# Softmax attention: which PSUM banks hold the maxima and which the scores, and where a step's side work stands

## The chip, the cores and the metric

The kernel runs on one core of a Trainium2 chip, in one launch. The metric is the device time in microseconds (us), the median of the runs.

## What is computed

The reference is a two-layer model; only its first attention matters here. For x of 8 x 512 x 128 (normalised by rows first), with 16 heads of 8:

```
q, k, v = split_heads(binlinear(x, Wq, bq)), ...      # binarised weights
att = softmax(einsum('bhtd,bhsd->bhts', q, k) * 8 ** -0.5)
y = einsum('bhts,bhsd->bhtd', att, v)                 # then binlinear(y, Wp, bp)
```

Behind it come a routed expert layer (8 experts, the best 2 of each token), a second attention with squared scores, and a coupling network.

## The kernel before

The attention is `attention0`. Its work is cut into **128 steps** (`LAST`), 16 for each of the 8 batch elements (`b` is the element, `t` the step in it). A quad is four heads (`GH = 4`) of one element; four steps make a quad, and step `s` handles one tile of 128 keys of it. The stacked queries and keys of a quad's four heads lie in four strips of 32 partitions, so that matmuls of the four heads use four different row strips of TensorE.

Each step has these parts:

- **maxima** (`maximum`, L616 to L627): TensorE computes the scores of 128 queries against all 512 keys, a bank of PSUM for each head, and VectorE reduces each to the negated maximum of every query (L1042). They run `AHEAD = 6` steps ahead of the scores. When a quad's 16 maxima are there VectorE transposes them (`turn`, L1047), and SyncE copies them into an extra row of the stacked queries (`max_rows`, L333), so that the scores come out with the maximum taken off.
- **scores** (`scores`, L629 to L641): 128 keys against 512 queries, one matmul for a head; ScalarE's exponential (L819) reads them.
- **weights** (`weigh`, L650 to L663): the exponentials of two steps before (`LAG = 2`) times the values, summed into the bank `av`, 4 heads beside each other, in two parts.
- **side work** at fixed steps: the gather of the sums by head at t = 2 and 4 (`gather`, L674), the turn of the normalised values at t = 6 (`turn_y`, L686), the output projection at t = 8 (L694), the projections of the queries and keys three elements ahead at t = 10 and 12 (`q_k`, L579), the next values at t = 14 (`values`, L587), and once each the router's gates, logits and counts. ScalarE reads each of them out.

A step is two halves, which TensorE issues as (`group`, L643 to L647, and the loop from L758): maximum, two scores, maximum; weights part 0; maximum, two scores, maximum; side work; weights part 1. A group with what follows it up to the next group is called a **half-step** here.

PSUM has eight banks: three take the maxima in turn (`max_banks`: bank0, bank1, misc), four (`quad`) hold scores in two pairs, and one is `av`. The pairs are used by units, numbered in the order of their issue in the table `units`: a unit is two scores or one piece of side work, and takes a pair. `wait_bank` (L287) makes TensorE wait until the unit two before has been read; ScalarE reads a pair of scores with one exponential of 1024 elements. `unit_read` counts what ScalarE has read, `max_free` what VectorE has reduced.

```
wait(pe, max_free, n - 2)        # maximum n: the bank of maximum n - 3 has been reduced
wait(engine, unit_read, n - 1)   # unit n: the pair of unit n - 2 has been read
```

The chain from a gather to the turn of the values: ScalarE copies the gathered sums (L857), VectorE inverts the denominators (`invert_sums`, L1059) one step after the gather and behind that step's maxima, GpSimd multiplies (`scale_rows`, L521), and then `turn_y` may start (it waits for `yn_done`). ScalarE reads `av` into `osb` (`read_o`, L826) at the ends of t = 1 and t = 9; gather and weights wait for that (`o_read`).

## Time and profile before

| | |
|---|---|
| median of 3 runs (lowest to highest) | 981.44 us (981.0 to 982.44) |
| the profiled execution, its own time | 983.3 us |
| its span | 981.5 us |
| PE busy | 894.2 us (91%) |
| DVE busy | 679.1 us (69%) |
| ACT busy | 633.1 us (65%) |
| POOL busy | 380.9 us (39%) |
| exponentials, L819 | 257.3 us in 256 |
| maxima on DVE, L1042 | 337.5 us in 512 |

The shares are over the whole program; the attention's steps lie between 50 and 416 us of the span. PE is TensorE (PEld its weight loads), DVE VectorE, ACT ScalarE, POOL GpSimd. The two groups of maxima (the banks, 222.0 us, and misc, 115.5 us) are added in the last line. A busy PE counts every matmul from its start to its modelled end, so matmuls of different row strips that run together count once, and a PE that looks busy may still be waiting.

### The profile page before, as it was taken

To read this page: it belongs to the slowest core of one execution; us is meant where nothing else is said; L and a number is where in the kernel's file an instruction comes from. 1 tells how busy PE (TensorE), PEld (TensorE's weight loads), DVE (VectorE), ACT (ScalarE), POOL (GpSimd) and SP (SyncE) were. 2 spreads that over 40 slices of the span, in tenths; PEclk is the share of its full clock that TensorE was granted. 3 is DMA by queue.
4 is the path that set the end of the run, shared out by engine and by line. 5 is a ranking of instruction groups with operands and counts; after the bars stand their busy time and mean duration, and the time that the engine had idled before them with its cause. 6 is when DMAs were issued, how large, how long until landed. Compare 5 with 4: busy or idle time off the path is not lost. (4 is left out here: it accounts for less than half of the span.)

```text
span 981.5 us, 18238 instructions
## 1 busy us (share of the span) xinstructions
PE 894.2 (91%) x6642; PEld 466.6 (48%) x6642; DVE 679.1 (69%) x1253; ACT 633.1 (65%) x1152; POOL 380.9 (39%) x376
## 2 busy tenths in 40 slices
PE   4699999999999999989898978899689999999997
PEld 2334444444444444468788866322234444434443
DVE  7779989898888998423333358777857667766654
ACT  4568787778787887832222223567567778777875
POOL 4112141325454343015565531455636446644200
PEclk9579999999999999989999989989779999999999
DMA  7715625132323000146666361369977999999700
GB/s 223 258 30 211 238 84 200 64 140 84 116 90 110 27 26 27 51 121 195 200 200 202 107 201 56 87 105 139 137 82 76 102 115 103 103 100 115 87 13 22
DMA packets 81484, 114.03 MB, mean 116 GB/s; under 512 B 14482, under 2 KB 58516, under 8 KB 78964
## 3 DMA queue, kind: packets, MB, share of 16 engines
q1 hardware_dynamic: 74228, 94.62, 48.5%
q0 software_dynamic: 6352, 17.86, 5.3%
q8 instruction: 53, 0.87, 0.4%
q10 hardware_dynamic: 816, 0.39, 0.1%
q14 instruction: 35, 0.29, 0.1%
HBM read 56.00 MB, written 33.57 MB: 91 GB/s over the span
## 5 line engine op out<-in xcount | busy, mean ns | idle before, releaser
L819 ACT ACTIVATE a_probs<-quad 128x1024 f32<-128x1024 f32 x256 | 257.3, 1024 | 58.3 <-PE quad L639 50.7
L1042 DVE TENSOR_REDUCE a_nmax<-bank 128x1 f32<-128x512 f32 x342 | 222.0, 680 | 31.5 <-PE misc L626 16.2
L1909 ACT ACTIVATE a_late<-quad 128x256 f32<-128x256 f32 (+3 forms) x512 | 180.5, 463 | 38.6 <-PE quad L1678 37.6
L2064 DVE SCALAR_TENSOR_TENSOR a_late<-a_late,const 128x512 f32<-128x512 f32 x128 | 117.1, 923 | 76.2 <-ACT a_late L1909 75.9
L659 PE MATMUL av<-a_probs,a_va 128*32 128x256 f32 x2048 | 163.2, 392 | 4.4 <-ACT a_osb L826 4.4
L626 PE MATMUL bank<-k_stack,q_stack 24*128 24x512 f32 x342 | 147.7, 515 | 6.1 <-DVE a_nmax L1042 4.2
L639 PE MATMUL quad<-q_stack,k_stack 25*128 25x512 f32 x512 | 129.8, 502 | 0.3 <-DMA q_stack<-a_ntop 0.3
L1042 DVE TENSOR_REDUCE a_nmax<-misc 128x1 f32<-128x512 f32 x170 | 115.5, 679 | 13.7 <-PE bank L626 12.6
L1678 PE MATMUL quad<-q_stack,k_stack 96*128 96x256 bf16 (+3 forms) x512 | 104.1, 303 | 7.8 <-ACT a_late L1909 4.0
L1689 PE MATMUL av<-a_late,a_va 128*32 128x512 f32 (+3 forms) x1024 | 97.2, 452 | 8.2 <-DVE a_late L2075 7.2
L626 PEld LDWEIGHTS bank<-k_stack,q_stack 24*128 24x128 f32 x342 | 59.5, 188 | 86.4 <-DVE a_nmax L1042 59.3
L514 POOL DMA_INDIRECT sorted_rows<-x_rows,a_slot x64 | 62.5, 976 | 74.3 <-PE av L659 70.6
L626 PE MATMUL misc<-k_stack,q_stack 24*128 24x512 f32 x170 | 87.6, 515 | 1.8 <-DVE a_nmax L1042 1.7
L1407 DVE TENSOR_TENSOR m_hid<-m_act,quad 128x512 f32<-128x512 f32 x55 | 37.4, 684 | 74.5 <-PE quad L1336 31.5
L1678 PEld LDWEIGHTS quad<-q_stack,k_stack 96*128 96x128 bf16 x512 | 44.5, 98 | 88.0 <-ACT a_late L1909 62.2
L1610 POOL TENSOR_TENSOR a_rest<-a_full,a_parts 128x512 f32<-128x512 f32 x32 | 41.4, 1294 | 94.4 <-DVE a_parts L2056 93.5
L659 PEld LDWEIGHTS av<-a_probs,a_va 128*32 128x32 f32 x2048 | 41.2, 108 | 70.1 <-issue 37.7
L1378 ACT ACTIVATE m_act<-bank 128x512 f32<-128x512 f32 x55 | 32.8, 596 | 53.0 <-PE bank L1331 41.2
L1305 POOL DMA_INDIRECT expert_rows<-m_ob,m_xr x50 | 47.8, 957 | 30.8 <-DVE m_ob L1414 18.5
L1373 ACT ACTIVATE m_xt<-quad 128x256 f32<-128x256 f32 x39 | 14.8, 383 | 69.0 <-PE quad L1317 59.6
L626 PEld LDWEIGHTS misc<-k_stack,q_stack 24*128 24x128 f32 x170 | 32.0, 188 | 42.4 <-DVE a_nmax L1042 29.4
L639 PEld LDWEIGHTS quad<-q_stack,k_stack 25*128 25x128 f32 x512 | 47.8, 183 | 6.2 <-ACT a_probs L819 3.3
(288 smaller groups left out, 1390.8 us busy)
## 6 DMA issues: line engine op xcount, KB each, us to landing
spread<-a_parts SPq DMA_DIRECT2D x48, 256.0 KB
q_stack<-a_parts SPq DMA_DIRECT2D x96, 128.0 KB, 7.5
k_stack<-a_parts SPq DMA_DIRECT2D x96, 128.0 KB, 7.7
wu<-packed_weights SPq DMA_DIRECT2D x20, 384.0 KB
m_wu<-packed_weights SPq DMA_DIRECT2D x19, 384.0 KB
q_stack<-spread SPq DMA_DIRECT2D x7, 1024.0 KB
k_stack<-spread SPq DMA_DIRECT2D x7, 1024.0 KB
sorted_rows<-in_shape_constants POOLq DMA_DIRECT2D x5, 1040.0 KB, 6.5
```

Of the source, the lines that this page charges most:

```text
L514: pool.indirect_dma_start(S["sorted"], bass.IndirectOffsetOnAxis(ap=slot[k][:, t:t + 1], axis=0), S["rows"][:, t, :], None).then_inc(done, 16)
L626: pe.matmul(max_banks[n % 3][:, :], qs[b % 4][at, c, qt * P:(qt + 1) * P].bitcast(F32R), ks[b % 4][at, c, :].bitcast(F32R), start=True, st ...
L639: last = pe.matmul(pair_of(n)[:, k, :], ks[b % 4][at, c, kt * P:(kt + 1) * P].bitcast(F32R), qs[b % 4][at, c, :].bitcast(F32R), start=True ...
L659: last = pe.matmul(av[STRIP * j:STRIP * (j + 1), at], va[b % 2][:, kt, GH * j + c, :], probs[:, (GH * s + j) % PROBS, at], start=(kt == 0 ...
L819: act.activation(probs[:, at:at + 2, :], pair_of(n), ACT.Exp, scale=scale).then_inc(unit_read, 1)
L1042: dve.tensor_reduce(nmax[quad % 2][:, at:at + 1], max_banks[n % 3][:, :], AX_X, ALU.max, negate=True).then_inc(max_free, 1)
L1305: pool.indirect_dma_start(S["outcome"], bass.IndirectOffsetOnAxis(ap=to, axis=0), ob[u % NX][:, k, :], None).then_inc(returned[u % NX], 16)
L1610: pool.tensor_tensor(r[:, :], f[:, :], pt[:, 0, :], ALU.subtract).then_inc(rested, 1)
L1678: pe.matmul(quad[:, n % 4, kt * P:T], ks[par][:, h, kt * P:(kt + 1) * P], qs[par][:, h, kt * P:T], start=True, stop=True).then_inc(s_mm, 1)
L1689: last = pe.matmul(av[STRIP * j:STRIP * (j + 1), kt * P:T], va[par][:, kt, GH * g + j, :], probs[:, (64 * b + 4 * t + j) % 12, kt * P:T], ...
L1909: act.activation(probs[:, (64 * b + n) % 12, kt * P:T], quad[:, n % 4, kt * P:T], ACT.Square, bias=1.0, scale=0.25)\
L2064: dve.scalar_tensor_tensor(out=blocks, in0=blocks, scalar=1.0, in1=S["tri"][:, None, :].broadcast_to([P, GH, P]), op0=ALU.add, op1=ALU.mul ...
```

## The change

The banks change places. The maxima now take the four banks of `quad` in two pairs: `maxima` issues two matmuls, and VectorE reduces both with one instruction of 1024 elements into two columns. The scores and all side work take bank0, bank1 and misc, one bank each, in turn (`unit_banks`): a unit is one score or one piece of side work, and waits until the unit three before it has been read. ScalarE reads each score with an exponential of its own. A group is now two maxima, then two scores. The side work stands between the step's first group and weights part 0 (before: behind the second group), on ScalarE between the exponentials of the two groups; `read_o` keeps its place. `AHEAD` is 7. The logits become two units of one bank, the two counts share a bank.

```diff
-        max_banks = (S["bank"][0], S["bank"][1], S["misc"])
+        unit_banks = (S["bank"][0], S["bank"][1], S["misc"])
...
-        AHEAD = 6
+        AHEAD = 7
...
-        SINGLES = len(units)
         for s in range(LAST):
             b, t = s // 16, s % 16
             units += [("s", s, 0), ("s", s, 1)]
             if s in GATES_AT:
...
+            units += [("s", s, 2), ("s", s, 3)]
...
-        def pair_of(n):
-
-            return S["quad"][:, 2 * ((n - SINGLES) % 2):2 * ((n - SINGLES) % 2) + 2, :]
+        def max_pair(n):
+
+            return S["quad"][:, 2 * (n % 2):2 * (n % 2) + 2, :]
 
         def bank_of(n):
 
-            return S["quad"][:, n % 4, :] if n < SINGLES else pair_of(n)[:, 0, :]
+            return unit_banks[n % 3]
 
         def wait_bank(engine, n):
 
-            if n < SINGLES:
-                wait(engine, unit_read, n - 3)
-            elif n < SINGLES + 2:
-                wait(engine, unit_read, SINGLES)
-            elif units[n - 2][0:2] == ("gather", B - 1):
-                wait(engine, last_read, units[n - 2][2] + 1)
+            if n >= 3 and units[n - 3][0:2] == ("gather", B - 1):
+                wait(engine, last_read, units[n - 3][2] + 1)
             else:
-                wait(engine, unit_read, n - 1)
+                wait(engine, unit_read, n - 2)
 
         def read_by_now(u):
 
...
-                if m == 0 and k == 0:
+                if m == 0 and i == 0:
                     wait(pe, first_quad, STACK)
-                if (m == TT or (m % 16 == 0 and m > 0)) and k == 0:
+                if (m == TT or (m % 16 == 0 and m > 0)) and i == 0:
                     wait(pe, stacked[b % 2], STACK * (b // 2 + 1))
-                r = (k + 2) % GH
-                at = slice(STRIP * r, STRIP * r + HROWS)
-                wait(pe, max_free, n - 2)
-                pe.matmul(max_banks[n % 3][:, :], qs[b % 4][at, c, qt * P:(qt + 1) * P].bitcast(F32R),
-                          ks[b % 4][at, c, :].bitcast(F32R), start=True, stop=True).then_inc(max_mm, 1)
+                wait(pe, max_free, n - 1)
+                for k in range(2):
+                    r = 2 * (1 - i) + k
+                    at = slice(STRIP * r, STRIP * r + HROWS)
+                    last = pe.matmul(max_pair(n)[:, k, :], qs[b % 4][at, c, qt * P:(qt + 1) * P].bitcast(F32R),
+                                     ks[b % 4][at, c, :].bitcast(F32R), start=True, stop=True)
+                last.then_inc(max_mm, 1)
 
             def scores(s, i):
-                n = unit_no["s", s, i]
                 quad, kt = s // TT, s % TT
                 b, c = quad // NG, quad % NG
                 if kt == 0 and i == 0:
                     wait(pe, rows_in[quad % 2], ROWS * (quad // 2 + 1))
-                wait_bank(pe, n)
-                for k in range(2):
-                    j = 2 * i + k
+                for j in range(2 * i, 2 * i + 2):
+                    n = unit_no["s", s, j]
                     at = slice(STRIP * j, STRIP * j + HROWS + 1)
-                    last = pe.matmul(pair_of(n)[:, k, :], ks[b % 4][at, c, kt * P:(kt + 1) * P].bitcast(F32R),
-                                     qs[b % 4][at, c, :].bitcast(F32R), start=True, stop=True)
-                last.then_inc(unit_mm, 1)
+                    wait_bank(pe, n)
+                    pe.matmul(bank_of(n)[:, :], ks[b % 4][at, c, kt * P:(kt + 1) * P].bitcast(F32R),
+                              qs[b % 4][at, c, :].bitcast(F32R), start=True, stop=True).then_inc(unit_mm, 1)
 
             def group(s, i):
                 if s + AHEAD < LAST:
-                    maximum(s + AHEAD, 2 * i)
+                    maxima(s + AHEAD, i)
                 scores(s, i)
-                if s + AHEAD < LAST:
-                    maximum(s + AHEAD, 2 * i + 1)
 
             def weigh(s, part):
 
                 b, c, kt = s // 16, s % 16 // TT, s % TT
                 if part == 0:
-                    wait(pe, unit_read, unit_no["s", s, 1] + 1)
+                    wait(pe, unit_read, unit_no["s", s, GH - 1] + 1)
...
             for s in range(LAST):
                 b, t = s // 16, s % 16
                 group(s, 0)
-                if s >= LAG:
-                    weigh(s - LAG, 0)
-                group(s, 1)
                 if s in GATES_AT:
                     gates(GATES_AT.index(s))
                 if s == LOGITS_AT:
@@ -780,6 +771,9 @@
                 if t == VALUES_AT and b + 1 < B:
                     values(b + 1)
                 if s >= LAG:
+                    weigh(s - LAG, 0)
+                group(s, 1)
+                if s >= LAG:
                     weigh(s - LAG, 1)
             for s in range(LAST - LAG, LAST):
                 weigh(s, 0)
...
             def exps(s, i):
-                n = unit_no["s", s, i]
-                if i == 0:
-
-                    wait(act, av_mm, s - PROBS // GH + 1)
-                wait(act, unit_mm, n + 1)
-                at = (GH * s + 2 * i) % PROBS
-                act.activation(probs[:, at:at + 2, :], pair_of(n), ACT.Exp, scale=scale).then_inc(unit_read, 1)
+                for j in range(2 * i, 2 * i + 2):
+                    n = unit_no["s", s, j]
+                    if j == 0:
+
+                        wait(act, av_mm, s - PROBS // GH + 1)
+                    wait(act, unit_mm, n + 1)
+                    act.activation(probs[:, (GH * s + j) % PROBS, :], bank_of(n)[:, :], ACT.Exp, scale=scale).then_inc(unit_read, 1)
 
             def read_o(b, half):
                 wait(act, av_mm, 16 * b + 8 * half + 8)
...
             for s in range(LAST):
                 b, t = s // 16, s % 16
                 exps(s, 0)
-                exps(s, 1)
-                if t == LAG - 1 and b >= 1:
-                    read_o(b - 1, 1)
-                if t == 8 + LAG - 1:
-                    read_o(b, 0)
                 if s in GATES_AT:
                     store_gates(GATES_AT.index(s))
                 if s == LOGITS_AT:
@@ -952,6 +941,11 @@
                     read_counts()
                 if t == VALUES_AT and b + 1 < B:
                     read_v(b + 1)
+                exps(s, 1)
+                if t == LAG - 1 and b >= 1:
+                    read_o(b - 1, 1)
+                if t == 8 + LAG - 1:
+                    read_o(b, 0)
             read_o(B - 1, 1)
             read_y(B - 1)
...
 
-            def maximum(m, k):
-                n, quad, qt = GH * m + k, m // TT, m % TT
-                at = TT * ((k + 2) % GH) + qt
+            def maximum(m, i):
+                n, quad, qt = 2 * m + i, m // TT, m % TT
+                at = 2 * TT * (1 - i) + qt
                 wait(dve, max_mm, n + 1)
-                dve.tensor_reduce(nmax[quad % 2][:, at:at + 1], max_banks[n % 3][:, :], AX_X, ALU.max, negate=True).then_inc(max_free, 1)
+                dve.tensor_reduce(nmax[quad % 2][:, at:at + 2 * TT:TT], max_pair(n), AX_X, ALU.max, negate=True).then_inc(max_free, 1)
 
             def turn(quad):
-                wait(dve, max_free, GH * TT * (quad + 1))
+                wait(dve, max_free, 2 * TT * (quad + 1))
                 wait(dve, rows_in[quad % 2], ROWS * (quad // 2))
                 dve.transpose(ntop[quad % 2][:, :], nmax[quad % 2][:, :]).then_inc(turned, 1)
 
@@ -1050,8 +1044,7 @@
                 maximum(m, 0)
                 if m % TT == 0 and m > 0:
                     turn(m // TT - 1)
-                for k in range(1, GH):
-                    maximum(m, k)
+                maximum(m, 1)
 
             def invert_sums(b, u):
```

**TensorE, from a plain step into the step with the turn of the values** (t = 5 and 6; L626 is a maximum, L639 a score, L659 the weights, L686 the turn). Before:

```order
L626 MATMUL bank<-k_stack,q_stack 128x512
L639 MATMUL quad<-q_stack,k_stack 128x512 x2
L626 MATMUL misc<-k_stack,q_stack 128x512
L659 MATMUL av<-a_probs,a_va 32x256 x4
L626 MATMUL bank<-k_stack,q_stack 128x512
L639 MATMUL quad<-q_stack,k_stack 128x512 x2
L626 MATMUL bank<-k_stack,q_stack 128x512
L686 MATMUL quad<-const,a_yn 128x128 x4
L659 MATMUL av<-a_probs,a_va 32x256 x4
```

The same place in the changed kernel (there the lines are L623, L636, L653 and L680):

```order
L623 MATMUL quad<-k_stack,q_stack 128x512 x2
L636 MATMUL bank<-q_stack,k_stack 128x512 x2
L653 MATMUL av<-a_probs,a_va 32x256 x4
L623 MATMUL quad<-k_stack,q_stack 128x512 x2
L636 MATMUL misc<-q_stack,k_stack 128x512
L636 MATMUL bank<-q_stack,k_stack 128x512
L680 MATMUL bank<-const,a_yn 128x128 x4
L653 MATMUL av<-a_probs,a_va 32x256 x4
L623 MATMUL quad<-k_stack,q_stack 128x512 x2
```

Maxima go in pairs into `quad`, scores one by one into the three other banks, and the turn stands one half-step earlier: behind the first group of its step.

**ScalarE, the same element, the start of its steps** (L819 and L813 are exponentials). Before:

```order
L819 ACTIVATE a_probs<-quad 128x1024 x6
L826 ACTIVATE a_osb<-av 128x512
L819 ACTIVATE a_probs<-quad 128x1024 x2
L857 ACTIVATE a_gathered<-quad 128x288
L819 ACTIVATE a_probs<-quad 128x1024 x4
L857 ACTIVATE a_gathered<-quad 128x288
L819 ACTIVATE a_probs<-quad 128x1024 x4
```

Now:

```order
L813 ACTIVATE a_probs<-bank 128x512 x2
L820 ACTIVATE a_osb<-av 128x512
L813 ACTIVATE a_probs<-misc 128x512
L813 ACTIVATE a_probs<-bank 128x512
L851 ACTIVATE a_gathered<-bank 128x288
L813 ACTIVATE a_probs<-misc 128x512
L813 ACTIVATE a_probs<-bank 128x512 x2
L813 ACTIVATE a_probs<-misc 128x512
L813 ACTIVATE a_probs<-bank 128x512 x2
L813 ACTIVATE a_probs<-misc 128x512
```

Each exponential of 1024 is two of 512, and the copies of the side work (here the gathered sums) have two exponentials of their step before them and two behind.

## Rows read from the trace of the kernel before

**Rows 1.** Busy time by stretch: us, then each engine's busy time, TensorE's clock, DMA.

```profile
40.00:60.00 20.00, 18.12 (x63) 7.23 (x67) 14.60 (x26) 8.52 (x12) 0.00 (x0) 0.50 0.24 97
260.00:300.00 40.00, 39.42 (x373) 17.72 (x371) 35.42 (x63) 33.02 (x39) 19.81 (x22) 1.00 0.26 91
```

**Rows 2.** VectorE's maxima in order of time: start, us, what, idle before.

```profile
265.72 0.68 DVE L1042 TENSOR_REDUCE a_nmax<-misc 128x1 f32<-128x512 f32 x1
266.32 0.68 DVE L1042 TENSOR_REDUCE a_nmax<-bank 128x1 f32<-128x512 f32 x1
267.88 0.69 DVE L1042 TENSOR_REDUCE a_nmax<-bank 128x1 f32<-128x512 f32 x1 [0.88 <-PE misc L626]
```

**Rows 3.** TensorE in order of time: a plain half-step, one with a projection.

```profile
262.87 0.49 PE L626 MATMUL misc<-k_stack,q_stack 24*128 24x512 f32 x1
263.86 0.50 PE L626 MATMUL bank<-k_stack,q_stack 24*128 24x512 f32 x1
...
265.26 0.50 PE L626 MATMUL bank<-k_stack,q_stack 24*128 24x512 f32 x1
265.69 1.16 PE L694 MATMUL quad<-wT,a_full 128*128 128x128 f32 x8
266.78 0.64 PE L659 MATMUL av<-a_probs,a_va 128*32 128x256 f32 x8
267.35 0.50 PE L639 MATMUL quad<-q_stack,k_stack 25*128 25x512 f32 x2
```

**Rows 4.** The longest waits between 100 and 440 us: total us, times, longest.

```profile
PEld bank L626 <- DVE a_nmax L1042: 43.6, 110, 0.5
```

**Rows 5.** Groups by line and shape, of VectorE and of ScalarE: count, busy us, mean ns, idle before.

```profile
L1002 DVE TENSOR_REDUCE a_alpha<-a_probs 128x2 f32<-128x256 f32 x1 | 0.4, 419 | 4.3 <-DMA a_probs<-in_L_attn_Wk 4.3
L819 ACT ACTIVATE a_probs<-quad 128x1024 f32<-128x1024 f32 x256 | 257.3, 1024 | 58.3 <-PE quad L639 50.7 <-issue 1.4
L834 ACT ACTIVATE a_full<-quad 128x512 f32<-128x512 f32 x8 | 4.8, 597 | 4.5 <-PE quad L686 4.5
```

**Rows 6.** ScalarE in order of time, behind the scores of 267.35.

```profile
267.98 1.96 ACT L819 ACTIVATE a_probs<-quad 128x1024 f32<-128x1024 f32 x2 [0.50 <-PE quad L639]
269.84 0.59 ACT L826 ACTIVATE a_osb<-av 128x512 f32<-128x512 f32 x1
```

**Rows 7.** The second attention: squares that read single banks, and the matmul waiting for one.

```profile
749.18 1.09 ACT L1909 ACTIVATE a_late<-quad 128x512 f32<-128x512 f32 x2
749.84 0.10 PEld L1678 LDWEIGHTS quad<-q_stack,k_stack 96*128 96x128 bf16 x1 [0.40 <-ACT a_late L1909]
```

**Rows 8.** TensorE's other pieces of work in order of time: a query projection, a gather.

```profile
271.58 1.13 PE L579 MATMUL quad<-xnT,wT 128*128 128x512 f32 x2
387.60 1.25 PE L674 MATMUL quad<-a_sel,a_osb 128*128 128x144 f32 x8
```

**Rows 9.** The first and last scores, and the ends of two stretches between them.

```profile
50.42 0.79 PE L639 MATMUL quad<-q_stack,k_stack 25*128 25x512 f32 x2
63.77 0.50 PE L639 MATMUL quad<-q_stack,k_stack 25*128 25x512 f32 x2
404.34 0.50 PE L639 MATMUL quad<-q_stack,k_stack 25*128 25x512 f32 x2
414.35 0.50 PE L639 MATMUL quad<-q_stack,k_stack 25*128 25x512 f32 x2
```

**Rows 10.** TensorE held by the reading of the sums.

```profile
270.57 0.64 PE L659 MATMUL av<-a_probs,a_va 128*32 128x256 f32 x8 [0.26 <-ACT a_osb L826]
```

**Rows 11.** From the inversion of the sums to the turn of the values.

```profile
259.07 0.34 DVE L1059 RECIPROCAL a_rden<-a_gathered 128x32 f32<-128x32 f32 x1
259.50 0.62 POOL L521 TENSOR_TENSOR a_yn<-a_gathered,a_rden 128x256 f32<-128x256 f32 x1 [2.01 <-DVE a_rden L1059]
260.44 0.66 PE L686 MATMUL quad<-const,a_yn 128*128 128x128 f32 x4
```

More of the change, by code:

```diff
@@ L260, in attention0 @@
             if s == LOGITS_AT:
-                units.append(("logits", 0, 0))
+                units += [("logits", 0, 0), ("logits", 1, 0)]
             if s in FIRST_QK_AT:
@@ L751, in _ @@
             for s in range(-AHEAD, 0):
-                for k in range(GH):
-                    maximum(s + AHEAD, k)
+                for i in range(2):
+                    maxima(s + AHEAD, i)
                 if s < 3 - AHEAD:
@@ L1083, in choose @@
                 if n == 2:
-                    dve.wait_ge(route_step, 1)
-                    wait(dve, unit_read, unit_no["logits", 0, 0] + 1)
-                    dve.tensor_reduce(top[:, :], prob[:, :, :], AX_X, ALU.max).then_inc(route_step, 1)
+                    wait(dve, unit_read, unit_no["logits", 1, 0] + 1)
+                    dve.tensor_reduce(top[:, :], prob[:, :, :], AX_X, ALU.max).then_inc(route_step, 2)
                 elif n == 3:
```

32 lines of the change are left out of this document (16 added, 16 removed).

## The prediction

> **What bounds the kernel now.** I read the busy time by stretch first. Between 260 and 300 us, inside the attention's steps, VectorE is busy 35.4 of 40 us, ScalarE 33.0 and TensorE nearly always, at a granted clock of 1.00, 2.4 GHz [rows 1]: no engine has much to spare, so I went on to the engines in order of time. VectorE's maxima, when nothing holds them, start 0.60 us apart [rows 2], four to a step. TensorE is held by them: 110 times its next maximum waited for VectorE to free a bank [rows 4]. In a plain half-step the last maximum goes out at 262.87 and the next group starts at 263.86: **0.99 us is what TensorE itself needs** from the last matmul of a group to the first of the next [rows 3], against 2 x 0.60 = 1.20 us of VectorE. So plain half-steps are VectorE's. Where side work comes in, TensorE is late: the projection takes 266.78 - 265.69 = 1.09 us, 0.07 less than its busy 1.16 [rows 3], and VectorE then idles 0.88 us [rows 2]. The chain of waits ends in the second attention and tells nothing of this stage.
>
> **VectorE after the change.** The 256 maxima of 1024 elements are not in the trace. 256 elements take 419 ns and 512 take 680, so an element costs 1.02 ns [rows 2, 5]; a pair starts the next 0.60 + 0.52 = 1.12 us later, with bounds 1.02 (that slope alone, twice) and 1.20 (nothing saved). I take 1.12.
>
> **ScalarE after the change.** An exponential of 512 should last what a copy of 512 lasts, 0.597 us [rows 5]; two squares of 512 on end take 1.09, so that the second starts 0.49 behind the first [rows 7]. One of 1024 occupies 0.92 (the second of two starts at 267.98 + 1.96 - 1.02 = 268.92, `read_o` at 269.84) [rows 5, 6]. Two small ones cost 0.98, 0.06 more, some 15 us over 256 pairs. That lies beside other work, as ScalarE idles 7 us of 40 [rows 1]. The Trainium skill (Advanced Engine Details and Errata, TRN2 Errata) says to use tiles of 512 or 1024, because the latency is exposed between instructions. By it the split exponentials add those 15 us and the joined maxima take off 256 x 0.08 = 20, and the kernel would gain 5; the sum below doesn't go by it.
>
> **The new loop.** What decides is how soon a score's bank comes back. Scores rotate through three banks, two per half-step, so the second score of a half-step needs the bank that the first score of the half-step before left. Its loop: score to exponential 267.98 - 267.35 = 0.63 [rows 3, 6], exponential 0.60 [rows 5], release to the waiting matmul 0.06 (the square that starts at 749.18 lasts 0.60, and the load follows at 749.84) [rows 7]: **1.29 us**, more than TensorE's 0.99. If both scores of one half-step go out together, the second of the next waits until 1.29 and the first of the following goes out 1.0 behind it, at 2.29; its partner's bank has just come back (the exponential began at 1.63, and 1.63 + 0.66 = 2.29). So two half-steps take 2.29, on average **1.145 us**. VectorE's 1.12 lies just under that: the new bound is the ring TensorE, ScalarE, bank, with VectorE almost level.
>
> **Side work is then paid in full.** Now VectorE's lead soaks up part of it; a ring with no lead does not. A piece between groups makes its half-step 1.0 + its own time, and the three that follow take 3.58 us. Counted at full clock: 14 gathers at 1.17 (1.25 less the 0.08 overlap), 12 projections of queries or keys at 1.05 [rows 8], 7 turns at 0.58 [rows 11], 7 output projections and 7 values at 1.09 [rows 3], the counts 0.6: **48.9 us**, as before.
>
> **Two waits that get longer.** (1) *Turn of the values.* It moves up one half-step, but the inversion on VectorE stays behind the maxima of t = 5. Before, inversion at 259.07, GpSimd 259.50 to 260.12, turn 260.44: 0.3 us to spare [rows 11]. After, the last pair of t = 5 is issued at x; VectorE starts it at x + 0.53 (267.35 to 267.88) [rows 2, 3], the inversion comes 1.12 later, GpSimd 0.43 behind that and lasts 0.62, release about 0.1: x + 2.8. TensorE wants the turn at x + 1.29 + 0.43 = x + 1.72 (0.43 is from a group's last matmul to what follows, 265.26 to 265.69) [rows 3]. It stands **1.1 us**, 7 times: 7.7 us. What is queued behind it is weights part 0 and the whole next group, thus ScalarE and VectorE too. Bounds: 0 if VectorE is well ahead, 1.6 if it is a pair behind. (2) *Reading the sums.* `read_o` comes behind the second exponential of t = 1; the gather now wants it right behind the next group. Counted from that half-step's scores, the exponentials start at 0.63 and 1.12, `read_o` at 1.61; it ends at 2.20, and its release takes 0.14 (269.84 + 0.59 to 270.57) [rows 6, 10]: 2.34 against 1.72, 0.6 us of standing, 7 times, and the same 3 times at t = 10 in the elements that have no projection there: 6.0 us (before, 0.26 each [rows 10]). Bounds: 0.26 as now, and 0.9 if both exponentials are late.
>
> **The sum.** From the first scores at 50.42 to the last group at 414.35 the kernel before takes 363.9 us, of which the first six half-steps, at 1.2 GHz [rows 1], take 13.3 [rows 9]; I keep those. After: 13.3 + 249 x 1.145 = 285.1, + 48.9 + 6.0 + 7.7, + 2.0 as my allowance for VectorE's other work (transposes, inversions, routing) where no side work hides it = **363.0**, 0.9 us less. In this stands the tail, where no maxima are left: ten half-steps took 10.0 us there [rows 9], and the ring makes them 11.5. Before the first scores there are 14 pairs in place of 24 single maxima, one step more because of `AHEAD`: 15.7 against 14.4 us of VectorE; but pairs give it 1.12 us in hand where TensorE turns tiles between them, against an idle 0.88 each time as in [rows 2], and there are five such places, so I take -0.5 (bounds -1.5, and +2.3 for a whole step of two pairs more). The last exponentials end 0.1 later. Together **-1.3 us**. The larger `AHEAD` gives the copy of the maxima one step more, and nothing waited for it; the logits' two units and the shared bank of the counts cost nothing. GpSimd's sorting waits for the weights of each step and moves along. The expert layer starts when the attention ends.
>
> The profiled execution took 983.3 us with a span of 981.5, the median of the runs is 981.44; I put the difference on the median: **980.1 us**.
>
> **Rivals.** *Both exchanges are free (faster).* If VectorE runs ahead so that the turn doesn't wait, 7.7 us go: 972. For it: the turn has time to spare now [rows 11]; against: VectorE is level with the ring, not ahead. *The ring is longer (slower).* The mechanism is the release of a score's bank. If it takes 0.14 as after `read_o` [rows 10] and not 0.06, two half-steps take 2.37, and 249 x 0.04 = 10 us come on top: 990. It decides soon: the sum breaks even at a half-step of 1.150, a loop of 1.30 us against my 1.29. For it: every score now has its own wait and signal. *The pair saves nothing:* at 1.20 VectorE still bounds, 249 x 0.055 = 14 us: 994; against it the slope of the reductions. *The clock falls:* the many short waits could drop TensorE to 1.2 GHz at times, where a matmul of 512 takes 0.79 instead of 0.50 [rows 9] and a half-step so 1.8 instead of 1.145; ten of them would cost 7 us: 987. Against: it stayed at 1.00 with 110 such waits [rows 1, 4]. The Trainium skill (TensorE: Matmul & The Clock Gate, A second HAM failure mode: psum-queue depth-cycling) tells of a kernel whose cycling through PSUM banks made the clock oscillate; by that rule this rival would be more likely than the trace makes it.
>
> **How the numbers follow.** The forecast's own range, from the bounds above, is 976 to 984. What a measurement can tell from no change is about 0.2%, 2 us. Forecast 0.45 (0.12 of it faster by more, 0.24 within, 0.09 slower); free exchanges 0.24; longer ring 0.22; pair saves nothing 0.05; clock 0.04. So faster 0.36, same 0.24, slower 0.40. The range reaches to both main rivals, 971 to 991.
>
> **What would show it.** Pairs of maxima 1.12 us apart where VectorE is not held; plain steps of 2.29 us; TensorE's waits in the attention on ScalarE's exponentials, not on VectorE; exponentials of 0.60; a wait of 1.1 us before each turn of the values; the half-steps of the tail 1.14 and not 1.00. It is wrong if plain steps still take 2.40, if the turn doesn't wait, or if the change of time lies outside 30 to 417 us.

## The result, and the profile after

The changed kernel takes **991.6 us** (median of 20 runs, 984.5 to 1009.2), against 980.7 us of the kernel before in the same comparison (20 runs, 972.0 to 987.4): **1.0112 of it, 95% interval 1.0079 to 1.0145**. It is slower. The forecast was 980.1 us in a range of 971 to 991; the result lies just outside, on the side of the slower rivals. Three of the twenty runs, those over 1.5% above the fastest, are left out of the ratio; without them the median is 989.4 us. The profiled execution of the changed kernel took 998.25 us with a span of 996.4 and lies above its median, so its losses are those of one of the slower runs.

The groups of instructions of the changed kernel that answer to the exponentials and maxima of before [rows 5]: line, engine, operation, count, busy us, mean ns, idle before.

```profile
PE 900.2 (90%) x6642; PEld 465.7 (47%) x6642; DVE 662.9 (67%) x997; ACT 651.1 (65%) x1408; POOL 380.9 (38%) x376
...
L1036 DVE TENSOR_REDUCE a_nmax<-quad 128x2 f32<-128x1024 f32 x256 | 300.5, 1212 | 71.5 <-PE quad L623 71.3
L813 ACT ACTIVATE a_probs<-bank 128x512 f32<-128x512 f32 x341 | 193.6, 597 | 25.1 <-PE bank L636 11.4
...
L813 ACT ACTIVATE a_probs<-misc 128x512 f32<-128x512 f32 x171 | 102.0, 597 | 24.8 <-PE bank L636 21.7
```

The prices are as forecast: an exponential of 512 takes 0.597 us, and VectorE's whole busy time falls from 679.1 to 662.9 us, 16.2 less (the prediction's joined maxima take off 20), while ScalarE's rises from 633.1 to 651.1, 18.0 more (its split exponentials add 15). The 337.5 us that the table of before gives for the maxima adds two groups that overlap in time, so 337.5 less 300.5 is not what the pairs save; nor are the two groups of exponentials here to be added. Yet the stage is longer. From the first scores (48.82) to the last group of scores (428.98) it takes 380.2 us, where it took 363.9 [rows 9]; the forecast was 363.0. Behind the last scores the two profiles differ by 0.3 us, and the first scores come 1.6 us earlier. So the spans' difference of 14.9 us is in this stage: 16.2 more in it, less the 1.6 ahead of it. (Below, "the stage" is always this stretch, first to last scores, of the profiled execution. Some of the expectations count it about 7 us longer, to where the attention's work ends.)

**What stands before the turn.** TensorE in order of time, changed kernel, through the step with a turn of the values. Columns: start, us, engine, line, what, and in brackets the idle time before and who ended it.

```profile
262.22 0.49 PE L623 MATMUL quad<-k_stack,q_stack 24*128 24x512 f32 x2
262.22 0.65 PE L636 MATMUL bank<-q_stack,k_stack 25*128 25x512 f32 x2
264.17 0.63 PE L680 MATMUL misc<-const,a_yn 128*128 128x128 f32 x4 [1.30 <-POOL a_yn L517]
264.73 0.64 PE L653 MATMUL av<-a_probs,a_va 128*32 128x256 f32 x8
265.30 0.50 PE L623 MATMUL quad<-k_stack,q_stack 24*128 24x512 f32 x2
...
265.73 1.08 PE L653 MATMUL av<-a_probs,a_va 128*32 128x256 f32 x8
266.74 0.79 PE L623 MATMUL quad<-k_stack,q_stack 24*128 24x512 f32 x2
...
268.48 0.79 PE L623 MATMUL quad<-k_stack,q_stack 24*128 24x512 f32 x2
```

TensorE stands 1.30 us for GpSimd's multiplication. The bank isn't what it waits for: in run 3 below, a matmul into the same bank goes out 0.64 us behind the group. From 265.73 on everything takes longer: weights 1.08 us and not 0.64, a maximum 0.79 and not 0.50, and the half-step from 266.74 to 268.48 lasts 1.74 us. The chain behind that wait, on VectorE and GpSimd (it answers to [rows 11], and is as the prediction described it: the inversion behind the last maxima of t = 5):

```profile
261.88 1.18 DVE L1036 TENSOR_REDUCE a_nmax<-quad 128x2 f32<-128x1024 f32 x1
262.98 0.34 DVE L1052 RECIPROCAL a_rden<-a_gathered 128x32 f32<-128x32 f32 x1
```

```profile
263.40 0.62 POOL L517 TENSOR_TENSOR a_yn<-a_gathered,a_rden 128x256 f32<-128x256 f32 x1 [2.12 <-DVE a_rden L1052]
```

**What follows the turn.** Stretches of 25 us around each of the seven turns (they start at 118.23, 168.86, 217.80, 264.17, 311.69, 357.64 and 402.43): busy time and count of PE, PEld, DVE, ACT, POOL, then TensorE's granted clock (1.00 is 2.4 GHz, 0.50 is 1.2), DMA share and GB/s.

```profile
105.00:130.00 25.00, 22.56 (x171) 9.90 (x167) 16.34 (x20) 15.33 (x30) 3.19 (x5) 0.73 0.33 128
158.00:183.00 25.00, 23.50 (x200) 9.95 (x199) 18.95 (x25) 17.55 (x33) 4.44 (x5) 0.80 0.37 134
205.00:230.00 25.00, 23.54 (x221) 10.95 (x222) 19.81 (x24) 19.38 (x38) 6.91 (x8) 0.93 0.27 97
252.00:277.00 25.00, 23.70 (x219) 10.87 (x217) 18.05 (x20) 18.36 (x35) 9.39 (x10) 0.86 0.29 107
300.00:325.00 25.00, 23.49 (x215) 10.46 (x213) 18.25 (x20) 18.51 (x35) 10.07 (x13) 0.86 0.29 104
345.00:370.00 25.00, 23.27 (x220) 10.63 (x220) 19.09 (x21) 19.39 (x38) 10.13 (x12) 0.93 0.08 24
390.00:415.00 25.00, 23.69 (x202) 10.91 (x201) 16.62 (x18) 17.05 (x33) 5.46 (x6) 0.80 0.04 13
```

Each of the seven holds a part at half clock. The clocks missing from 1.00 add up to 1.09, times 25 us over 0.5: **54.5 us at 1.2 GHz**, 51 of them at the turns (starting during the wait or up to 1.9 us behind it) and 3.4 behind one more wait, of 1.15 us before the matmul of 106.76. In the kernel before there was none between 64 and 414 us. A half-step takes 1.74 us there in place of about 1.10 (258.94 to 262.22 are three of them), so 51 us cost some 51 x (1 - 1.10 / 1.74) = 19 us.

One more thing was as forecast: the first gather of an element waits 0.57 us for `read_o` (the first of the seven 0.33).

### The profile page after: what moved, and what is told of

Same layout as the page of the kernel before. It is cut to its first block and busy times, and to the rows that moved or that the text cites. A ratio compares the mean times of both kernels' runs of the same rounds, so it can differ in the third digit from the quotient of the medians.

```text
span 996.4 us, 18240 instructions
## 1 busy us (share of the span) xinstructions
PE 900.2 (90%) x6642; PEld 465.7 (47%) x6642; DVE 662.9 (67%) x997; ACT 651.1 (65%) x1408; POOL 380.9 (38%) x376
## 5 line engine op out<-in xcount | busy, mean ns | idle before, releaser
L1036 DVE TENSOR_REDUCE a_nmax<-quad 128x2 f32<-128x1024 f32 x256 | 300.5, 1212 | 71.5 <-PE quad L623 71.3
L813 ACT ACTIVATE a_probs<-bank 128x512 f32<-128x512 f32 x341 | 193.6, 597 | 25.1 <-PE bank L636 11.4
L653 PE MATMUL av<-a_probs,a_va 128*32 128x256 f32 x2048 | 173.9, 415 | 1.7 <-ACT a_osb L820 1.2
L636 PE MATMUL bank<-q_stack,k_stack 25*128 25x512 f32 x341 | 143.9, 524 | 1.1 <-ACT a_gathered L851 1.1
L623 PE MATMUL quad<-k_stack,q_stack 24*128 24x512 f32 x512 | 137.9, 541 | 5.8 <-DVE a_nmax L1036 3.8
L813 ACT ACTIVATE a_probs<-misc 128x512 f32<-128x512 f32 x171 | 102.0, 597 | 24.8 <-PE bank L636 21.7
L623 PEld LDWEIGHTS quad<-k_stack,q_stack 24*128 24x128 f32 x512 | 51.2, 198 | 122.9 <-DVE a_nmax L1036 62.5
L636 PE MATMUL misc<-q_stack,k_stack 25*128 25x512 f32 x171 | 91.0, 532 | 0.1
L653 PEld LDWEIGHTS av<-a_probs,a_va 128*32 128x32 f32 x2048 | 41.9, 111 | 71.0 <-issue 44.5
L636 PEld LDWEIGHTS bank<-q_stack,k_stack 25*128 25x128 f32 x341 | 57.2, 191 | 7.8 <-issue 2.5
L1365 ACT ACTIVATE m_xt<-quad 128x256 f32<-128x256 f32 x39 | 14.9, 384 | 68.3 <-PE quad L1309 61.0
L1297 POOL DMA_INDIRECT expert_rows<-m_ob,xr x28 | 26.9, 961 | 55.7 <-DVE m_ob L1406 50.6
```

The source lines that it names most:

```text
L623: last = pe.matmul(max_pair(n)[:, k, :], qs[b % 4][at, c, qt * P:(qt + 1) * P].bitcast(F32R), ks[b % 4][at, c, :].bitcast(F32R), start=Tru ...
L636: pe.matmul(bank_of(n)[:, :], ks[b % 4][at, c, kt * P:(kt + 1) * P].bitcast(F32R), qs[b % 4][at, c, :].bitcast(F32R), start=True, stop=Tru ...
L653: last = pe.matmul(av[STRIP * j:STRIP * (j + 1), at], va[b % 2][:, kt, GH * j + c, :], probs[:, (GH * s + j) % PROBS, at], start=(kt == 0 ...
L813: act.activation(probs[:, (GH * s + j) % PROBS, :], bank_of(n)[:, :], ACT.Exp, scale=scale).then_inc(unit_read, 1)
L1036: dve.tensor_reduce(nmax[quad % 2][:, at:at + 2 * TT:TT], max_pair(n), AX_X, ALU.max, negate=True).then_inc(max_free, 1)
L1297: pool.indirect_dma_start(S["outcome"], bass.IndirectOffsetOnAxis(ap=to, axis=0), ob[u % NX][:, k, :], None).then_inc(returned[u % NX], 16)
```

## The experiments

Two theories. **A:** the wait before the turn costs twice, once as 1.3 us of standing, seven times (about 7 us), and once more by the half clock that follows it (about 19 us); the new banks by themselves are a gain. **B:** the new layout of the banks is what is slow (its ring with no lead, its many short waits), and the clock falls with it or by itself. A third question came up on the way: what the depth `AHEAD` is worth. All kernels were timed in five rounds against the kernel before, on the same chip in each group; "ratio" is to that.

### 1. The turn put back

```diff
-                if t == TURN_AT and b >= 1:
-                    turn_y(b - 1)
...
                 group(s, 1)
+                if t == TURN_AT and b >= 1:
+                    turn_y(b - 1)
                 if s >= LAG:
                     weigh(s - LAG, 1)
```

(and in the same way the turn's place in `units` and `read_y` on ScalarE). Expected:

> The changed kernel with one thing undone: the turn of the values (and its read on ScalarE) stands behind the second group of t = 6 again. Theory A (the wait of 1.30 us before each turn also makes TensorE's clock fall): no wait before the turns, no stretch at 1.2 GHz in the attention but the one after 108 us, whose wait is another; 7 x 1.3 = 9 us of standing and some 17 us of clock go: about 970 us, a ratio of 0.99 to the kernel before. Theory B (the clock falls because scores now cycle through three banks with short waits, the turns' waits cost only themselves): the stretches at 1.2 GHz stay, 9 us go: 983 us.

Measured: 971.4 us, ratio **0.9895** (0.9857 to 0.9933), the stage 354.3 us. The same place:

```profile
250.28 0.50 PE L623 MATMUL quad<-k_stack,q_stack 24*128 24x512 f32 x2
250.28 0.49 PE L636 MATMUL misc<-q_stack,k_stack 25*128 25x512 f32 x1
250.42 0.50 PE L636 MATMUL bank<-q_stack,k_stack 25*128 25x512 f32 x1
251.07 0.63 PE L680 MATMUL bank<-const,a_yn 128*128 128x128 f32 x4 [0.16 <-POOL a_yn L517]
...
252.20 0.50 PE L623 MATMUL quad<-k_stack,q_stack 24*128 24x512 f32 x2
```

VectorE there, three pairs on end, (3.50 - 1.23) / 2 = 1.13 us apart:

```profile
252.74 3.50 DVE L1036 TENSOR_REDUCE a_nmax<-quad 128x2 f32<-128x1024 f32 x3 [0.32 <-PE quad L623]
```

The wait is 0.16 us here and 0.32 at most, and behind none of the seven turns does the clock fall. With the rest of the change in place, the kernel is faster than before by 1%. Theory B falls: the same banks and the same short waits hold 2.4 GHz, but for 3.4 us behind the one long wait that is left (1.15 us, at 105.78).

### 2. The inversion earlier, the turn where the change put it

```diff
-            def maxima(m):
+            def maxima(m, between=None):
                 maximum(m, 0)
                 if m % TT == 0 and m > 0:
                     turn(m // TT - 1)
+                if between is not None:
+                    between()
                 maximum(m, 1)
```

(`between` is `invert_sums` in the steps that have one.) Expected:

> The changed kernel, all positions on TensorE and ScalarE kept; only VectorE inverts the gathered sums between the two pairs of maxima of its step instead of behind them, which brings the values some 1.1 us earlier. Theory A: the wait before each turn shrinks from 1.30 to about 0.1 to 0.3 us, the clock stays up, 972 us. Theory B: 983 us with the stretches at 1.2 GHz still there.

Measured: 971.6 us, ratio **0.9895** (0.9862 to 0.9929), the stage 353.6 us. VectorE, where the inversion now stands between the step's two pairs:

```profile
247.64 0.20 DVE L1041 STREAM_TRANSPOSE a_ntop<-a_nmax 128x32 f32<-128x32 f32 x1
247.77 0.31 DVE L1054 RECIPROCAL a_rden<-a_gathered 128x32 f32<-128x32 f32 x1
248.00 2.29 DVE L1036 TENSOR_REDUCE a_nmax<-quad 128x2 f32<-128x1024 f32 x2
```

The turn keeps its new place, between the groups, and waits 0.17 us. So it is not the place of the turn that costs; it is the wait. Both cures give the same time.

### 3. The wait kept, and filled

A dummy matmul (128x512 in fp32, into the bank that the turn is about to take, which overwrites its result) goes ahead of the turn's wait.

```diff
                 wait_bank(pe, n)
                 if b < B - 1:
+                    pe.matmul(bank_of(n)[:, :], wT[:, 0:C], S["xnT"][:, 0:T], start=True, stop=True)
                     wait(pe, yn_done, 2 * b + 2)
```

> The changed kernel with one extra matmul of 128 x 512 in fp32 (a projection whose result is overwritten, 1.05 us at full clock) before the wait of each turn, in the bank that the turn then takes: TensorE works through most of the 1.30 us instead of standing. Theory A: the 9 us of waiting stay, the clock doesn't fall: 975 us. Theory B: as the changed kernel, 991 us. If the clock has no share at all, 991 us too.

Measured: 978.5 us, ratio **0.995** (0.9919 to 0.9982), the stage 361.2 us. TensorE at a turn:

```profile
252.58 0.64 PE L636 MATMUL bank<-q_stack,k_stack 25*128 25x512 f32 x2
253.22 1.12 PE L676 MATMUL misc<-xnT,wT 128*128 128x512 f32 x2
254.43 0.66 PE L681 MATMUL misc<-const,a_yn 128*128 128x128 f32 x4
```

This is 3 us above the 975 that was expected. The turn goes out at the same distance from its group as in the changed kernel (254.43 - 252.58 = 1.85 us, there 264.17 - 262.22 = 1.95), so the delay is still paid. But TensorE works during it, and the clock does not fall behind any of the turns. This splits the loss: the stage is 6.8 us longer than in run 1, **1.0 us for each of the seven delays**, and 19.0 us shorter than in the changed kernel, **which is the clock** (51 us at half clock less; by the price above, 19 us). 361.2 us is also within 2 us of the forecast's 363.0: the prediction had summed the kernel that this one is.

### 4. The same dummy before three turns of seven

Turns of elements 1, 3 and 5 filled, those of 0, 2, 4 and 6 not.

```diff
-                    pe.matmul(bank_of(n)[:, :], wT[:, 0:C], S["xnT"][:, 0:T], start=True, stop=True)
+                    if b % 2 == 1:
+                        pe.matmul(bank_of(n)[:, :], wT[:, 0:C], S["xnT"][:, 0:T], start=True, stop=True)
```

> The changed kernel with the dummy matmul (128x512 in fp32, into the bank that the turn takes) before the turns of elements 1, 3 and 5 alone; the turns of 0, 2, 4 and 6 still make TensorE stand 1.3 us. Theory A (the standing is what makes the clock fall, place by place): stretches at half clock behind the four unfilled turns and none behind the three filled ones, in the same execution; the time between that of all filled (ratio to before 0.995) and the changed kernel's own (1.011): about 1.003 to 1.006, 984 to 987 us beside 981. Theory B (the dummy matmuls help in some other way, or the clock falls by the load of the whole kernel): half-clock stretches at both kinds of turn, or at neither.

Measured: 986.1 us, ratio **1.0063** (1.0025 to 1.0101), the stage 370.1 us. The seven stretches around its turns (elements 0 to 6 in order; columns as above):

```profile
105.00:130.00 25.00, 22.56 (x184) 9.96 (x180) 17.71 (x21) 16.91 (x32) 4.48 (x7) 0.80 0.33 128
155.00:180.00 25.00, 24.68 (x232) 10.76 (x231) 20.90 (x28) 20.36 (x39) 5.19 (x6) 1.00 0.42 149
200.00:225.00 25.00, 23.70 (x234) 11.09 (x234) 20.52 (x23) 20.84 (x40) 7.56 (x8) 1.00 0.27 100
245.00:270.00 25.00, 24.92 (x236) 11.41 (x236) 19.79 (x21) 20.91 (x40) 10.52 (x12) 1.00 0.30 110
292.00:317.00 25.00, 23.13 (x216) 10.36 (x212) 19.36 (x20) 19.21 (x36) 10.73 (x13) 0.86 0.27 101
336.00:361.00 25.00, 24.33 (x242) 11.28 (x242) 19.93 (x22) 20.55 (x40) 10.43 (x12) 1.00 0.09 27
380.00:405.00 25.00, 23.70 (x201) 10.48 (x199) 16.21 (x18) 17.03 (x33) 5.45 (x6) 0.80 0.04 12
```

Within one execution the clock stays at 1.00 behind the filled turns (second, fourth, sixth line) and falls behind three of the four unfilled ones. The fourth unfilled one (third line, turn at 212.53) waited 1.30 us as well and kept its clock. The expectation of all four was too firm: the wait makes the fall likely, not certain. 27.3 us at half clock are 23.9 more than in run 3, which has 3.4 elsewhere; at 0.37 each that is 8.8 us, and the stage is 8.9 us longer than run 3's 361.2.

### 5 and 6. The turn alone moved in the kernel before, and then filled

In the kernel before, only the turn and its read go between the two groups (the same edit as in run 1, the other way); then the dummy on top.

> The kernel before, banks and all other positions kept, with only the turn of the values moved between the groups of t = 6. Theory A: TensorE stands about 1.4 us before each of 7 turns, the clock falls after it here too, with the old banks: 995 to 1000 us. Theory B: the clock stays at 2.4 GHz between 63 and 425 us; VectorE's lead soaks up part of the standing: 985 to 988 us.

> The kernel before with its turn moved up between the two groups (that run took 1.020 of before, with seven waits of 1.16 us and half-clock stretches behind three of them), and now the same dummy matmul before each of those turns. Theory A (standing and clock are two prices, and the dummy takes away the second): no half-clock stretch behind the seven turns, the waits still cost about 8 us in all: ratio 1.008 to 1.012, 989 to 993 us. Theory B (in this layout the loss is the order of ScalarE's reads, not the clock): ratio 1.018 or more.

Measured: ratio **1.0203** (1.0163 to 1.0244) without the dummy, 1002.5 us (expected 995 to 1000), and **1.0079** (1.0049 to 1.0109) with it, 986.3 us beside 979.7. The first has seven waits of 1.16 to 1.23 us before its turns; in its profiled execution, the fastest of its six (996.3 us), the clock fell at three of them (17 us in all, the stage 375.7 us). With the dummy it stays at 1.00 between 66 and 428 us, and the stage takes 370.7 us. Two of the stretches without the dummy, one with a fall and one without:

```profile
345.00:370.00 25.00, 23.57 (x234) 10.66 (x232) 20.91 (x38) 19.23 (x23) 11.22 (x12) 1.00 0.08 23
390.00:415.00 25.00, 23.79 (x198) 10.09 (x190) 17.79 (x31) 16.17 (x19) 5.44 (x6) 0.80 0.03 10
```

So a wait before the turn does harm of the same kind in the old layout of the banks, and needs nothing of the new one. The ratio with the dummy, 1.008, is the 6.8 us of delay alone.

### 7. The banks alone: all side work put back

The changed kernel with all of the side work behind the second group, in `units`, on TensorE and on ScalarE, as in the kernel before.

> The changed kernel with the whole of the side work (gathers, turn, projection, queries and keys, values, routing) put back behind the second group, so that of the change the exchange of the banks and the depth of 7 are left. With the turn alone put back, the kernel took 971.4 us against 984.0 before, and its attention stage 361.4 us against 370.7. Theory A (the exchange of banks alone shortens the half-step from about 1.15 to 1.10 us, and the place of the other side work is worth nothing, since TensorE is the busy engine at either place): 971 to 974 us, attention 361 to 364, no wait of more than 0.3 us before the turn. Theory B (part of those 12 us is the new place of the side work: behind the second group each piece meets a full ring of three banks and stands): 978 to 984 us. Theory C (the place between the groups costs, by the 0.57 us that each first gather stands for read_o): 966 to 969 us, and the wait of the gathers for read_o is gone.

Measured: 973.0 us beside 980.8, ratio **0.9922** (0.9894 to 0.9949), the stage 356.9 us with no fall in it. Theory A: the exchange of the banks (with the depth of 7) is the gain, 7 us of the stage. The place of the side work (356.9 against 354.3 in run 1) can't be told from nothing: the two intervals overlap.

### 8. The old banks with the side work between the groups

The kernel before, all side work but the turn moved.

> The kernel before, banks and depth as they were, with all side work but the turn and its read between the two groups. Theory A (the place is worth nothing, and the gathers then stand some 0.5 us each for read_o, with about 0.9 us before the first read of gathered rows where the routing is late): 984 to 990 us. Theory B (the place is what the changed kernel without its turn wait gains by): 973 to 978 us.

Measured: 984.5 us beside 980.8, ratio **1.0046** (1.0017 to 1.0074), the stage 367.8 us, 3.8 more than before. In that layout the new place costs a little: gathers then stand for `read_o` (0.2 to 0.3 us, seven times), and the first read of gathered rows comes before the routing is done with the tile it writes, so that TensorE stands 1.20 us at 111.11 and the clock falls for 6.8 us.

### 9. Depth 6 with the new banks

```diff
-        AHEAD = 7
+        AHEAD = 6
```

in the kernel of run 1.

> The changed kernel with the turn put back behind the second group, and the maxima 6 steps ahead and not 7. The prediction put the depth at 0.5 us. If the depth is worth nothing else: 970 to 973 us beside the 971.4 with 7. If the seventh step is what keeps the new bases of a quad from being late (rows into the query stack): a wait of the scores at the start of a quad, of 0.5 us or more in 32 quads, and 985 us or more.

Measured: 987.7 us, ratio **1.007** (1.0041 to 1.01), where depth 7 gave 0.9895: **some 17 us for one step of depth**, the stage 383.2 us. My 970 to 973 was wrong and the rival with 985 or more right, though not as it was put: not all quads wait a little, two wait long. TensorE at the start of a quad, and the longest waits between 60 and 420 us (total us, times, longest):

```profile
176.66 0.50 PE L623 MATMUL quad<-k_stack,q_stack 24*128 24x512 f32 x2
180.60 0.79 PE L636 MATMUL misc<-q_stack,k_stack 25*128 25x512 f32 x1 [3.44 <-DMA q_stack<-a_ntop]
```

```profile
PE misc L636 <- DMA q_stack<-a_ntop: 3.8, 2, 3.4
PE bank L636 <- DMA q_stack<-a_ntop: 3.7, 2, 3.5
```

The scores of a quad need the maxima as an extra row of the stacked queries, which VectorE transposes and SyncE copies. With a depth of 6 that copy is started two steps ahead of its use. From the transpose to the scores the kernel before mostly has 4.5 us, this run mostly 3.5 to 3.8 where it doesn't wait, and run 1 with its depth of 7 mostly 5.5 to 6.2. In the case shown the transpose came at 173.67 and the scores went out at 180.60, 6.9 us later. The shorter lead alone doesn't explain that: at the same quad the kernel before used its copy 4.0 us behind the transpose (167.97 to 171.96) without a wait. What also differs is how soon another load followed. Here GpSimd issued a load of 512 KB of packed weights 0.9 us behind SyncE's first piece of the copy (174.78 and 173.90), there 1.9 us behind it (170.09 and 168.19). At the other late quad, between 93 and 101 us, the engines moved 269 GB/s. That the copy was late because of these loads fits, but no run takes them away.

Each of the two waits (3.50 us at 100.21, 3.44 us at 180.60) came with 13.7 us at half clock. The profiled execution, 996.4 us, is one of the slower of this run, and also has a stretch of 17 us at half clock at the end of the stage, with no wait over 0.6 us ahead of it. Its stage is 29 us longer than run 1's, so it shows more than the 17 us of the medians:

```profile
414.00:431.00 17.00, 17.00 (x106) 5.04 (x102) 0.00 (x0) 11.15 (x21) 0.00 (x0) 0.55 0.28 73
```

### 10. Depth 7 with the old banks

> The kernel before with its maxima 7 steps ahead and nothing else. With the new banks, depth 6 took 987.7 us where depth 7 took 971 to 973, as SyncE's copy of the maxima came 3.4 us late at the start of two quads. Here the copy was late by 0.2 us twice. Theory A (in the old layout the copy is just in time, so the depth is worth nothing or the few tenths): ratio 0.998 to 1.001. Theory B (part of the 10 us that the new layout gains is the depth): ratio 0.996 or less.

Measured: 983.9 us beside 979.7, ratio **1.0038** (1.0005 to 1.0071); the stage takes 363.5 us, 0.4 less than before, and the first scores come at 52.56, 2.1 later [rows 9]. Neither number that I gave: in the old layout depth buys nothing in the stage and its prologue costs 2 to 4 us. So the depth is no part of the gain of itself. It belongs to the new banks: those make the steps shorter, which takes from the copy's time, and with them the longer prologue costs little (first scores at 47.29 with a depth of 6, at 47.66 in run 1 with 7).

### 11 and 12. Early inversion, gathers and turn a step later; then depth 8

```diff
-        GATHER_AT, TURN_AT, PROJECT_AT, QK_AT, VALUES_AT = (2, 4), 6, 8, (10, 12), 14
+        GATHER_AT, TURN_AT, PROJECT_AT, QK_AT, VALUES_AT = (3, 5), 7, 9, (10, 12), 14
```

on top of run 2; then `AHEAD = 8` as well.

> The changed kernel with the inversion of the sums between the two pairs of maxima, and gathers, turn and projection each one step later (3, 5, 7 and 9). The run with the inversion alone took 971.6 us and still showed seven waits of 0.3 to 0.6 us of the first gather for read_o and one of 1.14 us behind the first read of gathered rows, which waits for the routing, with a stretch of 3.4 us at half clock behind it. Theory A (both waits go with the later place): no stretch at half clock between 63 and the end of the attention stage, the stage 3 to 6 us shorter than 360.7, time 966 to 969 us. Rival (the ring of ScalarE sets the pace there in any case, so a wait of TensorE of 0.3 to 0.6 us is refilled): 970 to 972 us.

> The kernel with early inversion and gathers, turn and projection a step later (968.2 us, 0.987 of before), with the maxima 8 steps ahead. If depth 7 already covers SyncE's copy everywhere: the same, 0.985 to 0.990 (the prologue has one step more of maxima, some 2 us, and the end one less). If the copy is still late in some executions with 7: 0.983 or less.

Measured: 968.2 us, ratio **0.9871** (0.983 to 0.9912), the stage 352.6 us; with depth 8, 968.8 us, **0.9893** (0.9852 to 0.9933), the stage 354.1. Neither shows a fall of the clock between 68 us and the end of the stage, so the one behind the first read of gathered rows is gone in these two executions. The stage is 1.0 us shorter than run 2's, where 3 to 6 were expected; the gain over run 2 (0.9895) lies inside the intervals, and 0.6 us of wait for `read_o` has moved to the weights: the rival for that part isn't refuted. Depth 8 adds nothing to 7. With run 11 the kernel beats both, by 1.3% the one before and by 2.4% the changed one (0.9871 / 1.0112).

## Why the prediction failed

**The step that failed** is the pair of sentences on two sides of it. "It stands **1.1 us**, 7 times: 7.7 us" priced the wait as standing and nothing else. And "*The clock falls* ... Against: it stayed at 1.00 with 110 such waits" weighed the rival, at 0.04, by waits that were not such waits. The 110 of before lasted 0.4 us each and 0.5 at most [rows 4]; no single wait of TensorE's matmuls in that stage reached half a microsecond. My own sum put seven of 1.1 us into it. Its price, 0.65 us for each half-step at the lower clock, was right (measured 0.64), but I supposed ten such half-steps where there were about thirty, and laid them to short waits, where run 1 shows that it is the long ones.

The trace of before could have raised the suspicion. Behind the last scores TensorE stands 1.00 us for the last turn and 1.36 us a little later, and then the clock falls:

```profile
421.15 0.63 PE L686 MATMUL quad<-const,a_yn 128*128 128x128 f32 x4 [1.00 <-DVE a_yn L1070]
...
425.05 1.09 PE L1317 MATMUL quad<-const,xr 128*128 128x128 f32 x4 [1.36 <-PEq L166]
```

```profile
425.00:432.00 7.00, 6.17 (x18) 4.75 (x19) 0.69 (x1) 3.01 (x6) 0.00 (x0) 0.52 0.70 220
```

I read the stage's own clock and did not look at what the clock does where waits of the length that I was adding already stand. It would have given odds and no certainty: between 420 and 740 us the kernel before has eleven waits of 1.14 us and more, and the clock fell at six of them. Between 435 and 565 us it stayed at 1.00 through four of them, of 1.35 to 1.62 us, in other work than the attention's:

```profile
525.65 0.44 PE L1317 MATMUL quad<-const,xr 128*128 128x128 f32 x2 [1.62 <-DMA xr<-sorted_rows]
```

```profile
435.00:565.00 130.00, 118.28 (x728) 107.15 (x727) 42.98 (x78) 36.89 (x76) 74.71 (x78) 1.00 0.59 182
```

**The other steps.**

- *Turn of the values, 1.1 us, 7 times:* it waited 1.29 to 1.45 us; the price of the delay alone was 1.0 us each (run 3 against run 1). Right, by the chain that was given; VectorE began the pair 0.73 us behind its issue (261.15 to 261.88) where the chain had 0.53, which is the rest.
- *Reading the sums, 0.6 us, 10 times:* 0.57, nine times, and 0.33. Right.
- *The sum of the stage without the clock:* forecast 363.0, measured 361.2 (run 3); without the wait 363.0 - 7.7 = 355.3 against 354.3 (run 1). Right within 2 us, and the plain half-steps of run 1 last 1.14 us on average, as forecast; but the engine that sets this pace was the other one. The ring was a little too long: in the tail, where there are no maxima, ten half-steps from 418.05 to 428.98 take 1.09 us each, not 1.145, in part because the exponential starts 0.57 us behind a lone score (258.94 to 259.51) and not 0.63. VectorE's pairs, at 1.13 us where I had 1.12, are thus the slower of the two. The waits say so too: TensorE's next maxima waited 124 times for VectorE, its scores three times for an exponential (its weights 55 times). "TensorE's waits in the attention on ScalarE's exponentials, not on VectorE" was wrong, and harmless, since the two lie within 0.04 us.
- *The first scores, -0.5 us:* -1.6.
- *Depth:* "gives the copy of the maxima one step more, and nothing waited for it". Nearly true of the kernel before (two quads waited 0.16 and 0.18 us for it) and misleading for the changed one. Had the change left it at 6, the same sum would have been wrong by 17 us more (run 9).
- *Rivals:* "both exchanges are free" (972) is what the kernel does once the wait is gone (971), though by the turn's place or an earlier inversion, not by VectorE running ahead. "The ring is longer" and "the pair saves nothing" are both refuted by 354.3 us in run 1. "The clock falls" is what happened.

The maxima and the waits of the changed kernel between 60 and 420 us, for the two readings above:

```profile
PEld quad L623 <- DVE a_nmax L1036: 52.2, 124, 0.7
...
PE bank L680 <- POOL a_yn L517: 8.0, 6, 1.5
```

```profile
418.05 0.50 PE L636 MATMUL bank<-q_stack,k_stack 25*128 25x512 f32 x1
...
428.98 0.74 PE L636 MATMUL bank<-q_stack,k_stack 25*128 25x512 f32 x2
```

## What to carry to other kernels

When a change gives TensorE a single wait that is longer than any it has in that stage, price it twice: as standing, and as a possible stretch at half clock behind it. Look for how often the second came where waits of that length already stand in the trace, and give it a chance and not a certainty. If the wait can't be taken away, a dummy matmul in it pays; here it took back three quarters of what the wait cost (1.0112 to 0.995, where no wait gives 0.9895). And when a loop gets quicker, recount in microseconds every distance that is written in steps, with room for a slow transfer: a copy that was just in time at a depth of 6 was 3.4 us late at two quads once the new banks had taken some 0.7 us of its lead and it met other loads.

## What the runs showed of the hardware

**Single waits and the clock.** Over the profiled executions of the changed kernel and all twelve experiments, TensorE's waits of 1.14 us and more, from 64 us to the last scores of the stage, number 27: eight in the changed kernel, one each in runs 1, 2, 3 and 8, seven in run 5, five in run 4 and three in run 9. With 21 of them the granted clock fell to 0.50, during the wait or close behind it. No other wait there was longer than 0.7 us, and beside those the clock fell twice, both in run 9: at 320.2 us for 3.4, with no wait over 0.3 us close ahead of it, and at 415.8 for 17.1, 2.3 us behind a wait of 0.58. Nothing between 0.7 and 1.14 us occurred, and what decides between the 21 and the 6 was not tried. That the falls vary from one execution to the next fits the changed kernel's spread of 25 us, where the six of run 12 (depth 8) lie within 4: its slowest run, 1009.2 us, had a mean granted clock of 0.914, the two fastest 0.941 and 0.949.

The Trainium skill (TensorE: Matmul & The Clock Gate, A second HAM failure mode: psum-queue depth-cycling) puts the changing clock of a bf16 kernel down to small idle times between groups of matmuls as they cycle through PSUM banks. Here that isn't what does it: run 1 cycles through the same banks as the changed kernel, with as many short waits (138 for VectorE between 60 and 440 us), and stays at 1.00 but behind its one long wait. The same page (Part 4: PE-mode transpose) says that transposes don't count as work for the clock. A turn is four of them, so this could have been a part of the cause; but the falls behind the waits of runs 1 and 8 come with no turn near, and turns that were filled (run 3) or had no long wait (runs 1 and 2) have none. No run tried turns without transposes.

**A reduction over two banks.** One `tensor_reduce` of 1024 elements in two banks lets its successor start 1.13 us later, two of 512 take 1.20 [rows 2]: 18 us less in 256 pairs, beside 16.2 less busy time of VectorE in all. An exponential of 512 reads its bank for 0.597 us, and two on end 1.09 us, against 1.024 for one of 1024: 17 us more in 256 pairs, beside 18.0 more busy time of ScalarE in all, which lay beside other work.
